# Squares of twenty tiles moved from ScalarE to GpSimd, and VectorE's taps of neighbouring tiles taken in turns

## What is computed

```python
x = x + _L0_attn_ref(_layernorm(x), Wq, Wk, Wv, Wb, Wa, A_log, dt_bias, Wo, conv_q, conv_k, conv_v)
...
def _causal_conv_silu(x, w):           # w: (channels, 4)
    xp = jnp.pad(x, ((0, 0), (3, 0), (0, 0)))
    return silu(sum(w[:, j] * xp[:, j:j + T, :] for j in range(4)))
q = l2_norm(_causal_conv_silu(x @ Wq.T, conv_q).reshape(B, T, 16, 64))
k = l2_norm(_causal_conv_silu(x @ Wk.T, conv_k).reshape(B, T, 16, 64))
v = _causal_conv_silu(x @ Wv.T, conv_v).reshape(B, T, 16, 128)
# then a gated delta-rule recurrence over time with q, k, v, alpha, beta; RMS norm; product with Wo
```

## Time and profile before

| | us |
|---|---|
| median of 3 runs | 1274.16 (1272.65 to 1280.89) |
| the profiled execution, its time | 1278.91 |
| its span, first to last instruction | 1277.1 |
| TensorE busy | 1109.0 (87%) |
| VectorE busy | 902.2 (71%) |
| ScalarE busy | 808.4 (63%) |
| GpSimd busy | 564.4 (44%) |

### The profile page before, as it was taken

One profiled execution on the slowest core, in us unless ns is written; L12 is line 12 of the kernel. 1 busy time (PEld: TensorE's weight loads), 2 busy tenths in 40 slices (PEclk: granted clock), 3 DMA queues, 4 the chain that ended last, 5 costly groups with the idle time before them and its releaser, 6 DMA issues.

```text
span 1277.1 us, 36892 instructions
## 1 busy us (share of the span) xinstructions
PE 1109.0 (87%) x14528; PEld 798.7 (63%) x14528; DVE 902.2 (71%) x1818; ACT 808.4 (63%) x1488; POOL 564.4 (44%) x1193
## 2 busy tenths in 40 slices
PE   5667899999999999999989989986879878798990
PEld 1123576776677676667767767775545445698990
DVE  4757689997899998899976787784457567152231
ACT  5786788887998897897876676663334333232430
POOL 1004366666566666666755664654010103104404
PEclk9989799999999999999998999998699888898995
DMA  4012262222222212222213222311001103398982
GB/s 151 1 49 69 49 164 54 56 72 53 51 65 55 58 45 78 53 54 72 54 45 83 62 54 71 66 37 30 10 14 22 28 9 125 112 295 285 335 292 54
DMA packets 131661, 106.33 MB, mean 83 GB/s; under 512 B 60112, under 2 KB 119376, under 8 KB 131232
## 3 DMA queue, kind: packets, MB, share of 16 engines
q1 hardware_dynamic: 129440, 99.76, 27.8%
q0 software_dynamic: 2048, 4.20, 1.0%
HBM read 84.06 MB, written 15.73 MB: 78 GB/s over the span
## 4 chain that ended last, share of the span: by engine, by line
PE 50%; DVE 24%; issue 10%; ACT 6%; POOL 5%; DMA 3%; SPq 2%; DVEq 0%; POOLq 0%; ACTq 0%
PE bank L1051 6%; PE pair L731 5%; DVE vc L1500 4%; DVE kc L1500 4%; PE bank L1058 3%; PE pair L695 3%; PE bank L1005 3%; DVE AM L1570 3%; PE bank L878 2%; PE bank L833 2%; PE bank L783 2%; POOL xs L1997 2%; DVE X L1654 2%; PE pair L849 2%; PE bank L772 2%
## 5 line engine op out<-in xcount | busy, mean ns | idle before, releaser
L1954 POOL TENSOR_TENSOR SU<-SU 128x14 f32<-128x14 f32 (+6 forms) x448 | 151.1, 337 | 35.1
L1950 POOL TENSOR_TENSOR SU<-SU 128x14 f32<-128x14 f32 (+6 forms) x448 | 149.6, 334 | 34.9
L1500 DVE SCALAR_TENSOR_TENSOR vc<-vy,conv,vc 128x512 f32<-128x512 f32 x192 | 152.8, 796 | 16.8 <-ACT vc L1193 16.4
L1500 DVE SCALAR_TENSOR_TENSOR kc<-ky,conv,kc 128x512 f32<-128x512 f32 x162 | 125.7, 797 | 10.0 <-ACT kc L1167 8.3
L2020 POOL TENSOR_TENSOR RR<-RR,nh 128x8 f32<-128x8 f32 x32 | 65.1, 2036 | 150.0 <-DVE RR L1642 149.9
L1836 DVE TENSOR_TENSOR vy<-bank,vc 128x512 f32<-128x512 f32 x46 | 31.8, 692 | 98.5 <-PE bank L1051 97.2
L731 PE MATMUL pair<-SM,KQ 64*128 64x128 f32 (+1 forms) x512 | 75.0, 370 | 20.3 <-DVE AM L1570 14.1
L1926 POOL TENSOR_TENSOR st<-st,nh 128x4 f32<-128x4 f32 x16 | 18.9, 1180 | 148.1 <-DVE st L1476 110.3
L695 PE MATMUL pair<-xnT,WQ 128*128 128x512 f32 x128 | 76.6, 682 | 0.2 <-DVE SM L1519 0.2
L663 PE MATMUL pair<-xnT,WQ 128*128 128x512 f32 x128 | 70.3, 634 | 5.9 <-ACT qb L1167 5.1
L1799 DVE TENSOR_REDUCE SM<-pair 128x4 f32<-128x1024 f32 x32 | 39.1, 1222 | 40.4 <-PE pair L963 40.3
(11 more groups left out here) (316 smaller groups left out, 3154.9 us busy)
## 6 DMA issues: line engine op xcount, KB each, us to landing
AM<-in_wex_dram SPq DMA_DIRECT2D x32, 768.0 KB, 5.6
SM<-dscr SPq DMA_DIRECT2D x58, 256.0 KB, 3.8
V<-in_wex_dram SPq DMA_DIRECT2D x14, 768.0 KB, 5.1
et<-dscr SPq DMA_DIRECT2D x38, 256.0 KB, 3.8
SM<-fscr SPq DMA_DIRECT2D x64, 128.0 KB, 2.9
scratch<-AM SPq DMA_DIRECT2D x128, 48.0 KB, 1.8
SU<-scratch SPq DMA_DIRECT2D x256, 15.5 KB
xs<-idle SPq DMA_DIRECT2D x2, 1472.0 KB, 9.4
```

Of the source, the lines that this page charges most:

```text
L1500: e.scalar_tensor_tensor(c, y[:, :, k:k + 256], conv[:, ct, k:k + 1], c, ALU.mult, ALU.add).then_inc(s_c, 1)
L1950: e.tensor_tensor(tmp[:, 0:k, 0:15 - k], sub[:, 0:k, k:k + 1].to_broadcast([128, k, 15 - k]), sub[:, k:k + 1, k + 1:16].to_broadcast([128, ...
L1954: e.tensor_tensor(sub[:, 0:k, k + 1:16], sub[:, 0:k, k + 1:16], tmp[:, 0:k, 0:15 - k], ALU.subtract).then_inc(s_su, 1)
```

## The change

`ksq` leaves ScalarE's queue in the opening, and a new function `square(t)` on GpSimd makes the same squares as a product of the tile with itself, for the twenty tiles of the opening; `norm(("l0", 1))` stands between those of tiles 5 and 6. In the main loop the squares stay on ScalarE. On VectorE the opening's iteration `t` becomes: tap 0 of tile `t`, tap 2 of tile `t - 1`, tap 1 of tile `t`; tap 2 of the last tile follows behind the loop.

```diff
             def ksq(t):
                 e.wait_ge(s_kfin, t + 1)
-                if 4 <= t < NK0:
-                    e.wait_ge(s_ksel, t - 3)
+                if t == NK0:
+                    e.wait_ge(s_ksq, NK0)
                 e.activation(squares_of(t).rearrange("p (b t) -> p b t", b=2), KQ[:, (t // 2) % RK, :, t % 2, :], ACT.Square).then_inc(s_ksq, 1)
...
                 if t:
                     ksilu(t - 1)
-                if t >= 2:
-                    ksq(t - 2)
...
             ksilu(NK0 - 1)
-            ksq(NK0 - 2)
-            ksq(NK0 - 1)
             exp_ahead()
...
             for t in range(NK0):
-                kconv(t)
+                kconv(t, [0])
+                if t:
+                    kconv(t - 1, [2])
+                kconv(t, [1])
...
                 if t == NK0 - 3:
                     lengths1(0)
+            kconv(NK0 - 1, [2])
             lengths(0)
...
+            def square(t):
+                e.wait_ge(s_kfin, t + 1)
+                if t >= 4:
+                    e.wait_ge(s_ksel, t - 3)
+                a = KQ[:, (t // 2) % RK, :, t % 2, :]
+                e.tensor_tensor(squares_of(t).rearrange("p (b t) -> p b t", b=2), a, a, ALU.mult).then_inc(s_ksq, 1)
+
...
-            norm(("l0", 1))
+            for t in range(NK0):
+                if t == 6:
+                    norm(("l0", 1))
+                square(t)
             scaled(0)
             causal(0)
```

## The result

The median went from 1273.41 us (4 runs, 1272.52 to 1280.89) to 1284.12 us (4 runs, 1282.55 to 1292.0). The ratio is 1.0096, with a 95% interval of 1.0058 to 1.0133: slower, by 10.7 us between the medians (their quotient is 1.0084) and by 7 to 17 us in the interval. The forecast was 1283.6.

What follows compares the result with a forecast made beforehand. The opening's waits between nearly even ScalarE and VectorE were what mattered. A tile going from 2.24 to 3.24 us made lengths1(0) 7.5 late and lengths2(0) 9.4 late: 1274.16 + 9.4 = 1283.6 us, range 1275 to 1293.

Steps and rivals of the forecast that it cites:

- The ring: Opening: ScalarE and VectorE wait for each other in turn once a tile, 3.24 us where it was 2.24.
- The square's length: GpSimd in the opening: each square takes 1.28 us; the period is 1.97 plus its length once over 1.26.
- the first rival: Opening: longer GpSimd squares drag the ring further, to 1286.1 or 1293.5 us, slower by over 1%; chance 0.2.
- The schedule: Opening, tile by tile from silu 1: gates and norms added to the ring's pace, lengths1(0) 7.5 us late.
- GpSimd against VectorE: Opening: a tap issued during a GpSimd product ends 0.55 us after it, adding 0.01 us a tile.
- The tail: End of the opening: table load and logarithm now follow silu 17, so lengths2(0) ends 9.4 us late.
- rival 3: Main loop's first passes give part of the delay back, 3 to 6 us remaining: 1277 to 1280; chance 0.07.
- Rival 2: Opening: no ring, VectorE's 1.98 us a tile sets the pace, faster than before at 1270.5 us; chance 0.07.
- The size: Whole kernel: 9.4 us added to the median of 1274.16, giving 1283.6 us, 0.7% more.

Runs made afterwards that it cites:

- e1: Kernel before with only the taps in turns on VectorE, squares left on ScalarE; silus 3.76 us apart, opening 87.5 us, ratio to before 1.0134.
- e6: Changed kernel with GpSimd clearings in place of each square, sums of squares constant; silus 3.24 us apart, opening 77.7 us, one run.
- e3: Changed kernel with ScalarE's copy of tile t+1 queued ahead of silu t-1; silus 2.77 us apart, ratio to before 1.0059.
- e7: Changed kernel with copy t+1 queued ahead of silu t-1 and GpSimd clearings for squares; silus 1.99, then 1.7 to 3.9 us apart, one run.
- e9: Changed kernel with every square made twice on GpSimd; silus 3.99 us apart, opening 89.7 us, one run.
- e2: Changed kernel with taps back in the old order, squares still on GpSimd; silus 3.11 us apart, opening 76.3 us, ratio to before 1.0042.
- e5: Changed kernel with taps in the old order and GpSimd clearings for squares; silus 2.24 to 2.46 us apart, opening 67.0 us, one run.
- e10: Kernel before with only the squares of tiles 3 and 4 on GpSimd; opening 69.6 us, ratio to before 0.9993.

## Why the prediction held, step by step

- **The ring.** Forecast 3.24 a tile, measured 3.24 to 3.25, each link within 0.01. e1 puts the square into it and finds 0.52 more; e6 takes GpSimd's reading out and finds nothing less; e3 and e7 open it on ScalarE's side and find 2.77 and 1.99. This is shown.
- **The square's length** was mis-sized: 1.28 forecast, 1.04 measured. It changed nothing in the ring, since from 1.26 down it ends before tap 0 needs the port; the 0.01 that the forecast adds for the port has thus nothing behind it. With 1.04 the first rival was farther off than I thought; its slope was right (e9).
- **The schedule.** From silu 1 to the end of `lengths2(0)` the forecast has 90.07 - 24.84 = 65.2, measured 66.6. Tiles 2, 3 and 4 took 3.24, 3.62 and 3.24 (forecast 3.24, 3.61, 3.24), the stretch over the gates 9.90 (9.89). The missing 1.4 lies in four places where I counted other VectorE work at nothing or at its old length: 0.15 at the norm's statistics (tile 6), 0.49 at its scaling (tile 8: L1484 took 1.83 beside a square that began at 51.54; its four instructions took 1.11 before), 0.66 at the second gate part (tile 10: 6.31 against 5.65, with L1525 at 1.15 instead of 0.48), and 0.1 at the tail. The second and third are again GpSimd's squares against VectorE: e6, which has the ring and no squares, has an opening 1.15 shorter than the changed kernel, most of it in these two (tile 8 in 3.24 instead of 3.73, tile 10 in 5.86 instead of 6.31; the 0.21 that e6 still has over the forecast's 5.65 is L1525 beside a clearing, 0.69 instead of 0.48). So the step that failed in size was "GpSimd against VectorE": I weighed it for the taps in the ring and not for the other instructions that stand beside squares.
- **The tail.** Table load behind silu 17, logarithm, `lengths2(0)`: forecast 1.9 more than the shift of `lengths1(0)`, measured 1.8 (84.72 to 90.09 is 5.37, before 76.35 to 79.90 was 3.55). `lengths(0)` stayed hidden behind the DMAs: TensorE was idle for 1.20 before the Gram product.
- **The loop gives nothing back that the medians show:** 10.4 in the opening, 10.7 between medians. The traces say nearly the same of the loop itself. Counted from silu 1, its first scaled keys (L1962) are 10.4 later than before, the fourth 12.0, the fifth 9.3 and the last of the 32 9.2 (845.82 against 837.25): at most 1.2 came back there, not the 3 to 6 of rival 3. The two profiled executions differ by only 4.5 at their ends; the other 4 went behind the loop, in parts that the change doesn't touch, and the medians don't show them.
- **Rival 2** was wrong by mechanism, though half of what it says is true: e7's 1.99 a tile is the 1.98 it reckons with, once ring and port are away.
- **The size.** 9.4 forecast, 10.4 in the opening, 10.7 between the medians: right to 1.3 us. That 1283.6 lies 0.5 from the measured median is partly luck, since the median it started from, 1274.16, moved to 1273.41 with a fourth run.

The Trainium skill (SBUF — State Buffer, Who interferes with whom) has GpSimd's reads exclude a VectorE instruction with two SBUF inputs, and its clearings not; e2 and e5 agree, with taps of 1.63 in the one and 0.75 in the other. It also counts `tensor_scalar`, with one SBUF input, among the instructions that can contend, namely in a mode that takes the whole pair; the 1.83 and 1.15 above agree, and so do the 1.49 and 0.69 beside the clearings of e6. What I priced by one stretched tap was thus right as a rule, and it applied in more places than I used it.

## What to carry to other kernels

Before two engines' queues are reordered, write down for one turn of the loop who waits for what, the in-order queues included, and look for a closed path: its length is the new pace, and freed engine time doesn't shorten it. A head start of one tile is lost by one instruction placed ahead of the one that finishes the last tile. Work moved to GpSimd is free only where VectorE has a gap as long as it; ask it of every VectorE instruction beside it, and ask what of GpSimd's work reads SBUF. Work that only writes left the taps alone here, but not every VectorE instruction (e6).

## What the runs showed of the hardware that I had not expected

- A product of a 128x512 tile with itself took GpSimd 1.04 us; the product of two different tiles took 1.26 to 1.28. That the equal operands make the difference is not tested.
- A tap that meets a GpSimd product ends 0.54 to 0.55 us after it, whether it was issued 0.55 after the product's start, 0.09 after (e9) or 0.04 ahead of it (e2). So the tap issued first by 0.04 was the one that waited; a VectorE instruction issued 0.17 ahead of a square (L1522 of the changed kernel, 58.35) ran on, and the square waited.
- GpSimd's clearings, which leave taps at 0.75 us, stretched two kinds of `tensor_scalar`: 1.11 to 1.41 and 1.49, and 0.48 to 0.89 and 0.69 (e5, e6).
- TensorE's granted clock was 1.00 with 7.09 of 10 us busy (74 to 84 us of the changed kernel), and fell to 0.50 at other places of the same opening in one execution than in the next (e10 against before, 65 to 68 us). Where it moved a silu here, a copy had waited for TensorE.
